# One attention stage, three orders: the rotation ahead of the next root, the second projection behind the first scores, the mask first into its bank

## The chip, the cores and the metric

The kernel runs on one core of a Trainium2 chip. The metric is the device time of one execution in microseconds (us), the median of several runs. A core has five engines that run their own instruction streams and meet at semaphores: TensorE (PE, with its weight loads shown apart as PEld), VectorE (DVE), ScalarE (ACT), GpSimd (POOL) and SyncE (SP), which issues the transfers. TensorE runs at 1.2 or 2.4 GHz; a profile shows which one was granted.

## The reference

The program is a chain of four layers on a sequence of 2048 tokens of width 256: latent attention with 16 heads, a mixture of experts, a gated linear recurrence and a quantized feed-forward layer. The change lies in the attention alone:

```
x_n = layernorm(x)
cq  = rms_norm(x_n @ w_qa.T);  q = cq @ w_qb.T          # 16 heads of 128 + 64
ckv = x_n @ w_kva.T;  k_pe = rope(ckv[..., 64:]);  c = rms_norm(ckv[..., :64])
k_nope, v = split(c @ w_kvb.T)
scores = (q_full @ k_full.T) * scale;  scores[causal] = -inf
y = softmax(scores) @ v @ w_o.T
```

Both norms divide by a root of a mean square, and `rope` rotates pairs of columns by tabled sines and cosines.

## The kernel before

The tokens are 16 tiles of 128. The first stage (lines 160 to 540) makes, for eight pairs of tiles, the normalized latents in transposed form, split into a high and a low part, and beside that the products of weights that later stages use. The second stage is attention itself. Both stages write their order down as a list called `plan`. Every engine walks the same list and does its own share of each entry, in list order, so an entry's place in the list is its place on every engine's queue.

First stage. The list is built in slots s = 0 to 10. For pair n the entries are `xn` (DVE normalizes the inputs, n = s + 1), `x_turn` (PE transposes, ACT copies out, n = s), `latents` (PE multiplies with the latent weights, L483; ACT sums squares, L270 and L272; POOL takes the root in `rms`, L339 and L341; n = s - 1), `latn` (DVE multiplies by the root, L419 and L422; POOL rotates the keys in `rope`, L350 to L357, and splits in `split`, L362 and L364; n = s - 2) and `turned` (PE transposes the latents, L493 to L495; ACT and DVE split them; n = s - 3). `stats` (DVE, L394 and L397) serves four tiles. `unit` entries are twelve weight products: PE multiplies, ACT copies, DVE subtracts (L433, L437, L450, L451); `in_slot` says how many stand in which slot and `bank_of` which PSUM bank each uses. A unit waits until the one before it in its bank has been subtracted. `wqp` in slot 7 is a pair of wide scalings on ACT and a pair of wide subtractions on DVE. On POOL, `split` is followed for pairs 1 and 3 by `fold` (L369), which scales a weight that the units need. PE's `turned` waits for the rotated keys.

Second stage. A group is one query tile with four heads, 64 groups in all; groups of a late and an early tile alternate. `project` (five products L662 into bank pQ, ACT copies out at L760, POOL rotates at L849 to L856) and `turn` (four transposes L669, ACT L764, DVE L879) make a group's queries. `scores` is a chunk of up to 512 keys: three products (L683, L684, L688) into one of four banks, where in a head's last chunk, the diagonal one, a 128-column product of an identity with a mask (L686) adds the causal mask. DVE takes the maximum (L892), ACT the exponential (L772), which frees the bank. `probs` transposes (L701) and `values` multiplies with the values (L743 to L745, 65 columns each). There are 256 diagonal chunks, one for each tile and head; in the four earliest tiles a head has that one chunk only.

Of the kernel before, what the change touches and what calls it, by code (L numbers as in the profile page):

```python
# [25 lines left out]
P = 128  # L26
# [48 lines left out]
def build(nc, x, w_lat, w_qn, w_qpe, w_kn, w_v, w_o, q_ln, kv_ln, cos2, sin2, gw, wg, wu, wd, sel,  # L75
          l_in, l_gate, l_b, l_lam, qg, qu, qd, sg, su, sd, out):
    with ExitStack() as whole:
        sems = {}

        def sem(name):  # L80
            if name not in sems:
                sems[name] = whole.enter_context(nc.semaphore(name))
            return sems[name]
# [9 lines left out]
        def sb(ctx, name, shape, dt=F32, side="left"):  # L93
            return ctx.enter_context(nc.sbuf_tensor(own(name), shape, dt, side=side))

        def sbr(ctx, name, shape, dt=F32):
            return sb(ctx, name, shape, dt, "right")

        def ps(ctx, name, shape, dt=F32):
            return ctx.enter_context(nc.psum_tensor(own(name), shape, dt))  # L100
# [21 lines left out]
        with ExitStack() as first_use:  # L122
            lT_hi = sb(first_use, "lT_hi", [P, 3, T], F32R)
            lT_lo = sb(first_use, "lT_lo", [P, 3, T], F32R)
# [5 lines left out]
        identb = sb(whole, "identb", [P, P], BF16)  # L130
        maskb = sb(whole, "maskb", [P, P], BF16)
# [35 lines left out]
        with ExitStack() as att:  # L167
# [10 lines left out]
            with ExitStack() as pre:  # L178
                NPR = NT // 2
# [12 lines left out]
                latn = sbr(pre, "latn", [P, 3, 2, LAT])  # L192
# [8 lines left out]


                units = [("vo", j) for j in range(H // 2)] + [("wq", 0), ("wq", 1), ("wq", 2), ("wq", 3)]
                in_slot = {5: 1, 6: 1, 7: 1, 8: 2, 9: 3, 10: 4}
                plan = [("stats", 0), ("xn", 0)]
                n_units = 0
                for s in range(NPR + 3):
                    if s % 2 == 0 and s // 2 + 1 < NT // 4:
                        plan.append(("stats", s // 2 + 1))
                    if s + 1 < NPR:  # L210
                        plan.append(("xn", s + 1))
                    if s < NPR:
                        plan.append(("x_turn", s))
                    if 3 <= s:
                        plan.append(("turned", s - 3))
                    if 1 <= s <= NPR:
                        plan.append(("latents", s - 1))
                    if 2 <= s <= NPR + 1:
                        plan.append(("latn", s - 2))
                    if s == 7:  # L220
                        plan.append(("wqp", 0))
                    for _ in range(in_slot.get(s, 0)):
                        plan.append(("unit", n_units))
                        n_units += 1
                assert n_units == len(units)

                bank_of = [0, 0, 0, 0, 1, 2, 3, 0, 1, 2, 3, 0]
                ubank = [pa[:], pt[:], pl[0][:, 0, :], pl[0][:, 1, :]]
                with nc.Block() as block:

# [302 lines left out]
            with ExitStack() as loop:  # L533
# [15 lines left out]
                pS = [ps(loop, f"pS{b}", [P, BT]) for b in range(4)]  # L549
# [9 lines left out]
                tile_at = lambda p: tiles_in_order[groups[p // HG][0]]  # L559

                chunk = [(p, c, min(4, tile_at(p) + 1 - 4 * c)) for p in range(NP) for c in range(tile_at(p) // 4 + 1)]
                first = [next(n for n, k in enumerate(chunk) if k[0] == p) for p in range(NP)] + [len(chunk)]
# [1 line left out]
                LAG = 2  # L564


                plan = [("project", 0), ("turn", 0), ("project", 1)] + [("scores", k) for k in range(first[1])]
                later = []
                sums_due = []

# [34 lines left out]
                for p in range(1, NP):  # L605
                    n = first[p + 1] - first[p]
# [30 lines left out]
                with nc.Block() as block:  # L637

                    @block.tensor
                    def _(pe):  # L640
# [31 lines left out]
                        def scores(at):  # L672
                            p, c, n = chunk[at]
                            i, h = divmod(p, HG)
                            if c == 0:
                                pe.wait_ge(sem("q_hi"), i + 1)
                                pe.wait_ge(sem("q_lo"), i + 1)
                            if at >= 4:
                                pe.wait_ge(sem("exped"), at - 3)
                            w = max(256, n * P)  # L680
                            o, ks = pS[at % 4][:, 0:w], slice(c * BT, c * BT + w)
                            q_hi, q_lo = (q[:, i % 2, h * P:(h + 1) * P] for q in (qT_hi, qT_lo))
                            pe.matmul(o, q_hi, lT_hi[:, 2, ks], start=True, stop=False)  # L683
                            pe.matmul(o, q_hi, lT_lo[:, 2, ks], start=False, stop=False)  # L684
                            if c == tile_at(p) // 4:
                                pe.matmul(pS[at % 4][:, (n - 1) * P:n * P], identb[:], maskb[:], start=False, stop=False,  # L686
                                          skip_group_check=True)
                            pe.matmul(o, q_lo, lT_hi[:, 2, ks], start=False, stop=True).then_inc(sem("scored"), 1)  # L688

                        def bank_t(step):  # L690
                            n = t_index[step]
# [39 lines left out]
                        def values(at):  # L731
# [7 lines left out]
                            for k in range(n):  # L739
# [6 lines left out]
                            m.then_inc(sem("valued"), 1)  # L746

                        steps = {"project": project, "turn": turn, "scores": scores, "probs": probs, "values": values,
                                 "o_turn": o_turn, "sum": sum_, "x_turn": x_turn}
                        for step, at in plan:  # L750
# [398 lines left out]
        c = whole.enter_context(ExitStack())  # L1149
# [20 lines left out]
        with ExitStack() as banks:  # L1170
# [70 lines left out]
            plan = [("up", 0), ("up", 1), ("gate", 0), ("split", 0), ("gate", 1)] + [step for slot in slots for step in slot]  # L1241
# [458 lines left out]
```

## Time and profile before

| | |
|---|---|
| median of 3 runs | 1726.22 us (1725.79 to 1726.46) |
| profiled execution | 1726.31 us, of which the span of the trace is 1724.6 us |
| first stage, until the second one's first product | 99.36 us |
| second stage | 99.36 to about 1240 us |
| TensorE busy in the span | 1571.8 us, 91% |

A time in the profile is in us from the start of the span; a mean duration is in ns where it says so. The start of a row tells when an instruction began; what stands in brackets is the idle time of its engine before it and what ended it. TensorE's rows overlap, since products are pipelined, so the distance from one start to the next tells what a product costs. A row of the timeline merges neighbours of a line, their number stands behind the x.

### The profile page before, as it was taken

What the parts mean: (1) busy time and instruction counts of PE and PEld (TensorE: products, weight loads), DVE (VectorE), ACT (ScalarE), POOL (GpSimd) and SP (SyncE); (2) the same over time, 40 slices, a digit from 0 to 9 for tenths busy, and PEclk for the clock granted to TensorE, in tenths of its full rate; (3) what the DMA queues carried; (4) which work ended last, traced back from release to release, by engine and by line L of the source; (5) the groups of instructions that cost most, each with busy time, mean ns of one, the idle gap of its engine ahead of it and who ended that gap; (6) DMA issues with size and microseconds to landing.
All of it is one profiled execution on the core that took longest, in us unless ns stands there. A gap on an engine that the chain in (4) does not pass through costs nothing. (4 is left out here: it accounts for less than half of the span.)

```text
span 1724.6 us, 38029 instructions
## 1 busy us (share of the span) xinstructions
PE 1571.8 (91%) x14452; PEld 1328.2 (77%) x14452; DVE 1184.3 (69%) x2472; ACT 1021.2 (59%) x2009; POOL 307.3 (18%) x752
## 2 busy tenths in 40 slices
PE   5679999999999899999999999999938999988997
PEld 3458877788888778888888888888826878866886
DVE  3347777777777677788778778778755547476564
ACT  2336665666666566667667667667624455555573
POOL 4411111112111211121211121121010002020231
PEclk8789999999999999999999999999968999999999
DMA  7000000000000000000000000000012100000000
GB/s 217 1 1 2 2 2 1 2 2 1 2 2 2 2 2 2 1 2 2 2 2 2 2 2 2 2 2 2 2 40 73 49 1 1 1 28 13 1 25 25
DMA packets 27524, 22.47 MB, mean 13 GB/s; under 512 B 9660, under 2 KB 25148, under 8 KB 27220
## 3 DMA queue, kind: packets, MB, share of 16 engines
q1 hardware_dynamic: 27348, 20.05, 4.1%
q8 instruction: 120, 1.97, 0.5%
q14 instruction: 56, 0.46, 0.1%
HBM read 17.95 MB, written 2.10 MB: 12 GB/s over the span
## 5 line engine op out<-in xcount | busy, mean ns | idle before, releaser
L783 ACT ACTIVATE pT_hi<-pT 128x512 f16<-128x512 f32 (+3 forms) x640 | 341.5, 534 | 303.6 <-PE pT L701 302.2
L904 DVE TENSOR_TENSOR pT_lo<-pT,pT_hi 128x512 f16<-128x512 f32 (+3 forms) x640 | 387.8, 607 | 148.5 <-ACT pT_hi L783 141.6
L772 ACT ACTIVATE pr<-pS,nmx 128x512 f32<-128x512 f32 (+3 forms) x640 | 401.0, 627 | 25.8 <-DVE nmx L895 24.0
L892 DVE TENSOR_REDUCE cmx<-pS 128x1 f32<-128x512 f32 x576 | 339.2, 617 | 64.0 <-PE pS L688 59.0
L701 PE MATMUL pT<-ident,pr 128*128 128x128 f32 x2176 | 347.3, 276 | 16.4 <-DVE pT_lo L904 15.1
L701 PEld LDWEIGHTS pT<-ident,pr 128*128 128x128 f32 x2176 | 251.9, 140 | 48.7 <-ACT pr L772 24.5
L743 PE MATMUL pO<-c_hi,pT_hi 128*128 128x65 f16 x2176 | 265.6, 194 | 18.5 <-DVE O L922 17.8
L683 PE MATMUL pS<-lT_hi,qT_hi 128*128 128x512 f32 (+2 forms) x640 | 265.5, 415 | 3.1 <-ACT pr L772 3.1
L744 PE MATMUL pO<-c_lo,pT_hi 128*128 128x65 f16 x2176 | 266.4, 193 | 0.0
L745 PE MATMUL pO<-c_hi,pT_lo 128*128 128x65 f16 x2176 | 263.7, 192 | 0.0
L688 PE MATMUL pS<-lT_hi,qT_lo 128*128 128x512 f32 (+2 forms) x640 | 255.8, 400 | 0.0
L1307 PE MATMUL pGU<-lT_hi,W_all 128*128 128x512 f32 (+1 forms) x640 | 220.4, 403 | 16.1 <-ACT sgb L1387 12.1
L684 PE MATMUL pS<-lT_lo,qT_hi 128*128 128x512 f32 (+2 forms) x640 | 234.5, 366 | 0.0
L743 PEld LDWEIGHTS pO<-c_hi,pT_hi 128*128 128x128 f16 x2176 | 205.9, 97 | 28.6 <-ACT pT_hi L783 20.6
L744 PEld LDWEIGHTS pO<-c_lo,pT_hi 128*128 128x128 f16 x2176 | 204.1, 98 | 6.6
L745 PEld LDWEIGHTS pO<-c_hi,pT_lo 128*128 128x128 f16 x2176 | 205.3, 97 | 0.0
L1307 PEld LDWEIGHTS pGU<-lT_hi,W_all 128*128 128x128 f32 (+1 forms) x640 | 121.1, 189 | 47.3 <-ACT sgb L1387 16.3
L849 POOL TENSOR_TENSOR qt<-qs,sn 128x128 f32<-128x128 f32 x64 | 29.2, 457 | 687.5 <-ACT qs L760 687.5
L688 PEld LDWEIGHTS pS<-lT_hi,qT_lo 128*128 128x128 f32 x640 | 123.8, 193 | 16.7
L683 PEld LDWEIGHTS pS<-lT_hi,qT_hi 128*128 128x128 f32 x640 | 120.7, 189 | 16.8 <-ACT pr L772 2.9
L684 PEld LDWEIGHTS pS<-lT_lo,qT_hi 128*128 128x128 f32 x640 | 122.0, 191 | 11.0
L1307 PE MATMUL pGU<-lT_lo,W_all 128*128 128x512 f32 (+1 forms) x320 | 127.3, 398 | 0.0
(268 smaller groups left out, 2484.6 us busy)
## 6 DMA issues: line engine op xcount, KB each, us to landing
X<-in_x SPq DMA_DIRECT2D x4, 512.0 KB, 6.8
wo<-in_w_o SPq DMA_DIRECT2D x1, 2048.0 KB, 10.9
out<-X SPq DMA_DIRECT2D x8, 256.0 KB, 2.0
raw<-in_wd SPq DMA_DIRECT2D x14, 128.0 KB, 2.1
raw<-in_wg SPq DMA_DIRECT2D x13, 128.0 KB, 2.7
raw<-in_wu SPq DMA_DIRECT2D x13, 128.0 KB, 2.7
wqn<-in_w_qn SPq DMA_DIRECT2D x1, 1536.0 KB, 16.1
raw<-in_qg SPq DMA_DIRECT2D x6, 128.0 KB, 2.5
```

The costliest lines, as they stand in the source:

```text
L683: pe.matmul(o, q_hi, lT_hi[:, 2, ks], start=True, stop=False)
L684: pe.matmul(o, q_hi, lT_lo[:, 2, ks], start=False, stop=False)
L688: pe.matmul(o, q_lo, lT_hi[:, 2, ks], start=False, stop=True).then_inc(sem("scored"), 1)
L701: m = pe.transpose(o[:, k * P:(k + 1) * P], pr[:, at % RING, k * P:(k + 1) * P], ident[:])
L743: pe.matmul(o, hi, c_hi[:, j, 0:KVL + 1], start=(j == 0), stop=False)
L744: pe.matmul(o, hi, c_lo[:, j, 0:KVL + 1], start=False, stop=False)
L745: m = pe.matmul(o, lo, c_hi[:, j, 0:KVL + 1], start=False, stop=(j == tile_at(p)))
L772: act.activation(pr[:, at % RING, 0:n * P], pS[at % 4][:, 0:n * P], ACT.Exp, bias=nmx[:, p % 4:p % 4 + 1]).then_inc(sem("exped"), 1)
L783: act.activation(pT_hi[:, a % 4, 0:chunk[a][2] * P], src, ACT.Copy).then_inc(sem("t_hi"), 1)
L892: ch.inc(dve.tensor_reduce(cmx[:, p % 2, c:c + 1], pS[at % 4][:, 0:n * P], AX.X, ALU.max))
L904: dve.tensor_tensor(pT_lo[:, a % 4, 0:w], src, pT_hi[:, a % 4, 0:w], ALU.subtract).then_inc(sem("t_lo"), 1)
L1307: mm = pe.matmul(pGU[bank % 3][0:r, :], W_all[:, m, 2 * g + i, k * P:k * P + r], xT[j][:, k, ts], start=(q == 0), stop=(q == 5))
```

## The change

Three edits. In the first stage the entry `latn` of pair s - 2 moves from behind `latents` to the front of its slot; one unit moves from slot 10 to slot 4, with the banks renumbered. In the second stage `project` of group 1 moves behind the scores of the first head. In a diagonal chunk the mask's product comes first and opens the bank; the three others add to it.

```diff
-                in_slot = {5: 1, 6: 1, 7: 1, 8: 2, 9: 3, 10: 4}
+                in_slot = {4: 1, 5: 1, 6: 1, 7: 1, 8: 2, 9: 3, 10: 3}
                 for s in range(NPR + 3):
+                    if 2 <= s <= NPR + 1:
+                        plan.append(("latn", s - 2))
                     if s % 2 == 0 and s // 2 + 1 < NT // 4:
...
                     if 1 <= s <= NPR:
                         plan.append(("latents", s - 1))
-                    if 2 <= s <= NPR + 1:
-                        plan.append(("latn", s - 2))
...
-                bank_of = [0, 0, 0, 0, 1, 2, 3, 0, 1, 2, 3, 0]
+                bank_of = [0, 0, 0, 0, 0, 1, 2, 3, 0, 1, 2, 3]
...
-                plan = [("project", 0), ("turn", 0), ("project", 1)] + [("scores", k) for k in range(first[1])]
+                plan = [("project", 0), ("turn", 0)] + [("scores", k) for k in range(first[1])] + [("project", 1)]
...
-                            pe.matmul(o, q_hi, lT_hi[:, 2, ks], start=True, stop=False)
-                            pe.matmul(o, q_hi, lT_lo[:, 2, ks], start=False, stop=False)
-                            if c == tile_at(p) // 4:
-                                pe.matmul(pS[at % 4][:, (n - 1) * P:n * P], identb[:], maskb[:], start=False, stop=False,
+                            diagonal = c == tile_at(p) // 4
+                            if diagonal:
+                                pe.matmul(pS[at % 4][:, (n - 1) * P:n * P], identb[:], maskb[:], start=True, stop=False,
                                           skip_group_check=True)
-                            pe.matmul(o, q_lo, lT_hi[:, 2, ks], start=False, stop=True).then_inc(sem("scored"), 1)
+                            pe.matmul(o, q_hi, lT_hi[:, 2, ks], start=not diagonal, stop=False, skip_group_check=diagonal)
+                            pe.matmul(o, q_hi, lT_lo[:, 2, ks], start=False, stop=False, skip_group_check=diagonal)
+                            pe.matmul(o, q_lo, lT_hi[:, 2, ks], start=False, stop=True, skip_group_check=diagonal).then_inc(sem("scored"), 1)
```

On POOL in slot 2 of the first stage, where `ss` to `rr` is a root, `rt` and `latn` the rotation, `c_hi` and `c_lo` the split, and `rs` the deviation of the inputs:

```order
 L339 TENSOR_SCALAR ss<-ss 128x4
 L341 TENSOR_TENSOR rr<-ss,mhalf 128x2x2
+L350 TENSOR_TENSOR rt<-latn,sn 128x2x32
+L351 TENSOR_TENSOR rt<-latn,sn 128x2x32
+L353 TENSOR_TENSOR latn<-latn,cs 128x2x32
+L354 TENSOR_TENSOR latn<-latn,cs 128x2x32
+L356 TENSOR_TENSOR latn<-latn,rt 128x2x32
+L357 TENSOR_TENSOR latn<-latn,rt 128x2x32
+L362 CAST c_hi<-latn 128x2x64
+L364 TENSOR_TENSOR c_lo<-latn,c_hi 128x2x64
 L332 TENSOR_SCALAR rs<-mv 128x4
 L334 TENSOR_TENSOR rs<-rs,mhalf 128x4
```

Pair 0's rotation and split now stand directly behind pair 0's root, where before the root of pair 1 came first; every later pair is moved in the same way.

TensorE where the second stage begins, before, from the transposes of group 0's queries on (the products before them are group 0's projection):

```order
L669 MATMUL pQ<-ident,qs 128x128 x4
L662 MATMUL pQ<-W_hi,lT_hi 128x512
L662 MATMUL pQ<-W_lo,lT_hi 128x512
L662 MATMUL pQ<-W_hi,lT_lo 128x512
L662 MATMUL pQ<-W_1,lT_hi 128x512
L662 MATMUL pQ<-W_1,lT_lo 128x512
L683 MATMUL pS_1<-lT_hi,qT_hi 128x512
```

and in the change, from the first head's diagonal chunk on (three full chunks stand between the transposes and it):

```order
L685 MATMUL pS_1<-maskb,identb 128x128
L687 MATMUL pS_1<-lT_hi,qT_hi 128x512
L688 MATMUL pS_1<-lT_lo,qT_hi 128x512
L689 MATMUL pS_1<-lT_hi,qT_lo 128x512
L662 MATMUL pQ<-W_hi,lT_hi 128x512
L662 MATMUL pQ<-W_lo,lT_hi 128x512
L662 MATMUL pQ<-W_hi,lT_lo 128x512
L662 MATMUL pQ<-W_1,lT_hi 128x512
L662 MATMUL pQ<-W_1,lT_lo 128x512
L687 MATMUL pS_1<-lT_hi,qT_hi 128x512
L688 MATMUL pS_1<-lT_lo,qT_hi 128x512
L689 MATMUL pS_1<-lT_hi,qT_lo 128x512
```

Group 1's projection has changed places with the first head's scores, and stands between the first and the second head.

TensorE at a diagonal chunk of an early tile, behind the products with the values, before:

```order
L745 MATMUL pO<-c_hi,pT_lo 128x65
L683 MATMUL pS_1<-lT_hi,qT_hi 128x256
L684 MATMUL pS_1<-lT_lo,qT_hi 128x256
L686 MATMUL pS_1<-maskb,identb 128x128
L688 MATMUL pS_1<-lT_hi,qT_lo 128x256
L701 MATMUL pT_1<-ident,pr 128x128 x4
```

and in the change:

```order
L746 MATMUL pO<-c_hi,pT_lo 128x65
L685 MATMUL pS_1<-maskb,identb 128x128
L687 MATMUL pS_1<-lT_hi,qT_hi 128x256
L688 MATMUL pS_1<-lT_lo,qT_hi 128x256
L689 MATMUL pS_1<-lT_hi,qT_lo 128x256
L702 MATMUL pT_1<-ident,pr 128x128 x4
```

The mask's product has moved from the third place to the first; from here on every line of the program is one higher.

## Rows read from the trace of the kernel before

**Rows 1.** The page's part on engines: busy us, share of the span, instructions.

```profile
PE 1571.8 (91%) x14452; PEld 1328.2 (77%) x14452; DVE 1184.3 (69%) x2472; ACT 1021.2 (59%) x2009; POOL 307.3 (18%) x752
```

**Rows 2.** Windows: stretch, length, PE, PEld, DVE, ACT, POOL busy, clock, DMA share, GB/s.

```profile
30.00:60.00 30.00, 19.78 (x68) 13.01 (x67) 9.04 (x21) 9.58 (x40) 17.09 (x35) 0.77 0.18 42
130.00:680.00 550.00, 512.10 (x5590) 442.08 (x5587) 406.48 (x809) 352.72 (x697) 90.47 (x216) 1.00 0.01 2
680.00:1240.00 560.00, 550.50 (x6111) 479.94 (x6108) 445.58 (x955) 383.30 (x760) 100.50 (x240) 1.00 0.01 2
```

**Rows 3.** Timeline of slots 5 to 7, first stage: start, duration, instruction.

```profile
46.50 4.87 PE L483 MATMUL pl<-wl,xnT 128*128 128x384 f32 x8
...
51.83 0.20 ACT L272 ACTIVATION_READ_ACCUMULATOR junk<-pl 128x1 f32 x1
...
52.40 1.02 POOL L341 TENSOR_TENSOR rr<-ss,mhalf 128x4 f32<-128x4 f32 x1
...
55.23 0.32 POOL L357 TENSOR_TENSOR latn<-latn,rt 128x64 f32<-128x64 f32 x1
...
55.65 0.30 PE L493 MATMUL pk<-ident,latn 128*128 128x128 f32 x1 [2.98 <-issue]
...
56.33 2.75 PE L483 MATMUL pl<-wl,xnT 128*128 128x384 f32 x8
...
63.82 4.44 PE L483 MATMUL pl<-wl,xnT 128*128 128x384 f32 x8
```

**Rows 4.** Timeline of slots 2 to 8, what starts and bounds them.

```profile
19.68 0.42 DVE L419 TENSOR_TENSOR latn<-pl,rr 128x256 f32<-128x256 f32 x1 [3.48 <-POOL rr L341]
...
26.07 4.85 PE L483 MATMUL pl<-wl,xnT 128*128 128x384 f32 x8
...
35.57 2.35 POOL L369 TENSOR_TENSOR wv<-wv,kln 128x1024 f32<-128x1024 f32 x1
...
75.51 4.03 PE L483 MATMUL pl<-wl,xnT 128*128 128x384 f32 x8
```

**Rows 5.** Timeline from slot 7 to the second stage's first product.

```profile
72.36 1.28 DVE L437 SCALAR_TENSOR_TENSOR W<-wqp,qln,W 64x1024 fp32r<-64x1024 f32 x1
...
88.56 0.27 PE L493 MATMUL pk<-ident,latn 128*128 128x128 f32 x1
...
97.23 0.76 DVE L437 SCALAR_TENSOR_TENSOR W<-pa,qln,W 64x512 fp32r<-64x512 f32 x1 [1.03 <-ACT W L297]
...
99.36 0.77 PE L662 MATMUL pQ<-W_hi,lT_hi 128*128 128x512 f32 x1 [2.89 <-PEq L105]
```

**Rows 6.** Timeline of the second stage's beginning.

```profile
108.03 0.77 PE L662 MATMUL pQ<-W_hi,lT_hi 128*128 128x512 f32 x1 [1.50 <-DVE qT_lo L879]
...
110.54 0.60 ACT L760 ACTIVATE qs<-pQ 128x512 f32<-128x512 f32 x1 [3.38 <-PE pQ L662]
...
113.53 0.46 POOL L856 TENSOR_TENSOR qs<-qs,qt 128x128 f32<-128x128 f32 x1
...
115.22 0.69 ACT L772 ACTIVATE pr<-pS,nmx 128x512 f32<-128x512 f32 x1 [4.09 <-DVE nmx L895]
...
116.82 0.60 PE L669 MATMUL pQ<-ident,qs 128*128 128x128 f32 x4
```

**Rows 7.** Timeline of TensorE at a diagonal chunk; the last such row.

```profile
138.81 0.36 PE L683 MATMUL pS<-lT_hi,qT_hi 128*128 128x256 f32 x1
139.01 0.28 PE L684 MATMUL pS<-lT_lo,qT_hi 128*128 128x256 f32 x1
139.13 0.23 PE L686 MATMUL pS<-maskb,identb 128*128 128x128 bf16 x1
139.17 0.36 PE L688 MATMUL pS<-lT_hi,qT_lo 128*128 128x256 f32 x1
139.37 0.49 PE L701 MATMUL pT<-ident,pr 128*128 128x128 f32 x3
...
1201.10 0.48 PE L683 MATMUL pS<-lT_hi,qT_hi 128*128 128x512 f32 x1
```

## The prediction, made before the changed kernel ran

> **What bounds the kernel now.** I read the page first: TensorE is busy for 91% of the span, the next engine for 69% [rows 1]. That is an average, so the windows come next. In the second stage TensorE is busy 512 of 550 us in its first half and 550.5 of 560 in its second, at a granted clock of 1.00, the 2.4 GHz level [rows 2]. There TensorE is the limit, with some 38 us of idle time in the first half. In the first stage it is not: from 30 to 60 us it is busy 19.8 of 30 us, at a mean clock of 0.77, and no other engine is busier than 17.1 us [rows 2]. Nobody is full, so something there goes round in a ring.
>
> The timeline shows the ring [rows 3]. The reader should follow one slot: the latents start at 46.50 (8 products, 4.87 us); ACT has the squares at 52.03; POOL has the root at 53.42; then the rotation, until 55.55; at 55.65 PE starts the transposes, and at 56.33 the next latents. The rotation is that of the pair before: its own inputs were there a slot earlier, but in POOL's queue it stands behind a root that needs this slot's squares. So one slot costs 5.53 (latents and squares) + 1.39 (root) + 2.13 (rotation) + 0.78 (hand-over and transposes) = 9.83 us, one after the other. The next slot, 56.33 to 63.82, is the same ring with the latents in 2.75 instead of 4.87 us: 7.49 us. From slot 3 (26.07) to slot 8 (75.51 [rows 4]) five slots take 49.4 us.
>
> **The change, part by part.** *Rotation ahead of the next root.* The rotation of pair n now follows its own root and DVE's product with it (0.42 us [rows 4]), and no longer waits for the squares of pair n + 1. The dependences still close, but over two slots: latents and squares 5.53, root 1.39, DVE product 0.42, some 0.5 where that product stands behind a unit's subtractions, rotation 2.13, transposes 0.78: 10.75 us for two slots, 5.4 each. With the short latents, 5.53 becomes 7.49 - 1.39 - 2.13 - 0.78 = 3.19, and the ring 4.2 us a slot.
>
> Then another limit shows. TensorE's work in the window 30 to 60 is 19.8 us for three slots, 6.6 each at clock 0.77 [rows 2], hence 5.1 if all of it ran at the upper level and 10.2 if all at the lower. POOL's 17.1 us hold two folds of 2.35 [rows 4], so some 4.1 us a slot, under TensorE. I take 6.4 us a slot: TensorE almost without gaps, at a mean clock near 0.8, a little above today's, since its gaps of 3 us [rows 3] get shorter.
>
> DVE pays at the front. Its product with the root stands ahead of the statistics and the normalization in its queue. In slot 2 that product starts at 19.68 [rows 4] and both halves end near 20.7; the statistics of four tiles and the normalization of pair 3, done before it until now, follow it: some 2.6 us in all by my estimate, until 23.3. Behind that queue wait PE's transposes of the inputs (0.6), those of pair 0 (1.3) and the latents of slot 3, which I put at 25.2, against 26.07. Slot 7 begins at 25.2 + 4 x 6.4 = 50.8, against 63.82 [rows 3].
>
> Slot 7 holds the wide scalings. Before, DVE ended them at 73.64 [rows 5], 9.8 us after slot 7's latents began. Behind them on DVE now stand a unit's subtractions (0.85) and the product for pair 6; behind that POOL's rotation waits (2.1), and behind that PE's transposes: 50.8 + 9.8 + 0.85 + 0.42 + 2.1 = about 64. The root of pair 7 stands behind that rotation and its split in POOL's queue, so the last transposes come another 0.8 + 1.39 + 0.42 + 2.13 = 4.7 later, at 68.7. What follows took 99.36 - 88.56 = 10.8 us [rows 5] with four weight units; now there are three, and the one taken out, which moved into slot 9's wait, saves at most (97.23 - 88.56)/4 = 2.2; I take 1.9. The second stage then starts at 68.7 + 8.9 = 77.6 instead of 99.36: **22 us**. The moved first unit (slot 4) runs on PE where the 6.4 already counts it; its inputs need the fold, 2.35 us on POOL, now also a slot earlier, which I hold hidden; if that cover is gone, it is 2 us once. Bounds: with 5.1 us a slot the gain is 27 us, with 9 it is 12. No transfer binds: DMA is at 0.18 in the window 30 to 60 [rows 2], after which it carries nothing here.
>
> *Projection behind the scores.* Before, group 1's projection starts at 108.03, ACT copies it at 110.54, POOL has rotated it at 113.99, and PE transposes at 116.82; the first exponential starts at 115.22 [rows 6]. Now the four chunks of scores start at 108.03. They took from 110.30 to 114.1; with the low clock over more of them they end near 113.0. The projection follows, until about 114.2, and its copy ends near 114.9. ACT's queue has that copy ahead of the first exponential, which therefore begins at 114.95 instead of 115.22: nearly nothing won. The rotation takes 113.99 - 111.14 = 2.85 us after the copy and now ends at 117.75, so PE's transposes slip from 116.82 to 117.8. Behind them on PE and ACT wait the first transposes of probabilities and all further exponentials. That is a **loss of 1.0 us**; it lies between -0.3 (only the exponential counts) and +1.4.
>
> *Mask first.* The starts [rows 7] tell what a product costs. The first product behind a 65-column one takes 0.20 us to the next start, the second 0.12, the mask 0.04, the third, behind the mask, again 0.20. So a float32 weight load lies open for 0.08 us when the product ahead is short, and it is hidden behind a long one. Before, an early tile's diagonal chunk pays twice: behind the values and behind the mask. Now the mask's load, half as long, meets the short product, and one open load remains, behind the mask. Where a long product is ahead (the chunk before in the same head) the sum stays the same: one open load in either order. I count 76 of the 256 diagonal chunks behind short products in the trace, the first at 138.81, the last at 1201.10 [rows 7]. 76 x 0.08 = 6.1 us is the upper bound; below it is 0, should the mask's own load lie open instead, and less than 0 only for the rival below. Three quarters of these chunks lie in the first half, where TensorE idles 38 us of 550 and a faster PE partly just waits longer. I take half, **3 us**.
>
> One rule of the Trainium skill would make it nothing: the page "TensorE: Matmul & The Clock Gate", section "The mechanism" of its part on packing small matmuls, lists that a weight load overlaps products in flight only when the row group differs. All products here use all rows, so no load would hide and no place would be better: 3 us less gain, 1705. The distances of 0.12 against 0.20 us speak against it.
>
> Sum, against the profiled execution: 1726.31 - 22 + 1 - 3 = 1702.3. That execution lies 0.1 us from the median 1726.22, so the forecast is **1702 us**.
>
> **The rivals.** (a) The denser work does not lift TensorE's clock, or it falls for longer in the waits around the wide scalings. At 9 us a slot the first stage gains 12 us: 1726.3 - 12 + 1 - 3 = 1712, and up to 1716 without the mask's share. For it speaks that the clock was 0.77 with TensorE busy for two thirds. (b) The clock goes the other way, all slots at 5.1 us: 27 us, and the whole mask share of 6: 1694. The skill's page named above says in its table on why this matters for kernels that idle gaps between bursts of products lower the clock; shorter gaps would then mean more time at 2.4 GHz. (c) The mask brings nothing: 1705. It lies within my range. (d) The stage's gain is hidden or replaced: DVE's queue, where the product with the root now stands ahead of the normalization, feeds a new ring of one slot (root, product, normalization, transposes, latents). Worked out, that path needs 1.39 + 0.42 + 0.68 + 1.8 + 0.7 + 0.6 us behind the squares in the slots with statistics and has a whole slot for it, so I give it little: about 1726. (e) Slower: opening the bank with a 128-column product makes the wide product that adds onto it dearer. Above (22 - 1)/256 = 0.08 us for each of 256 chunks, the same size as the open load, it eats the gain. The second and third product add onto a bank already and take 0.12 us for 256 columns [rows 7], which speaks against it.
>
> **How the numbers follow.** A measurement of this kernel can tell about 0.2%, 3.5 us. The main case, with its mask share anywhere from 0 to 6, gets 0.74 and runs from 1695 to 1709; (a) 0.12, (b) 0.08, (d) 0.03, (e) 0.03. The range 1691 to 1713 takes in (b) and most of (a). Faster by over 0.2%: 0.95; within 0.2%: 0.03; slower: 0.02.
>
> **What would show it.** The second stage's first product near 77 us; starts of L483 six to seven us apart in slots 3 to 7; POOL's rotation directly behind DVE's product; near the beginning of the second stage the transposes L669 of group 1 about 9.8 us after the projection or scores begin; at early tiles the distances 0.04, 0.20, 0.12, 0.12. The prediction is wrong if the slots keep 9 us or more, if the exponentials do not slip with the transposes, or if the wide scalings of slot 7 move the end by more than 3 us against the 64 worked out.

## The result, and the profile after

The changed kernel takes 1701.31 us in the median of 4 runs (1700.4 to 1701.61), the one before 1726.01 in the runs beside it. The ratio is 0.9864, its 95% interval 0.9852 to 0.9877: 24.7 us less, where 24 were forecast. The profiled execution of the changed kernel took 1701.13 us with a span of 1699.4, against 1724.6.

The page of the changed kernel, the part on engines:

```profile
PE 1560.8 (92%) x14452; PEld 1309.5 (77%) x14452; DVE 1182.0 (70%) x2472; ACT 1020.6 (60%) x2009; POOL 306.5 (18%) x752
```

TensorE is 11 us less busy, though it does the same 14452 products. The mean granted clock of the whole execution rose from 0.972 to 0.977, so more of the products run at the upper level; how much of the 11 us that explains was not taken apart. Windows of the changed kernel (stretch, length, busy us of PE, PEld, DVE, ACT and POOL, granted clock, DMA share, GB/s):

```profile
30.00:60.00 30.00, 24.04 (x98) 15.89 (x97) 19.74 (x46) 17.54 (x65) 22.18 (x53) 0.94 0.17 40
88.00:94.00 6.00, 2.93 (x16) 1.75 (x14) 1.52 (x4) 1.98 (x4) 2.59 (x6) 1.00 0.00 0
95.00:101.00 6.00, 6.00 (x21) 4.64 (x22) 2.46 (x6) 1.76 (x4) 0.00 (x0) 0.50 0.00 0
```

Against [rows 2], all engines do more in the same 30 us of the first stage, and TensorE's clock there is 0.94 instead of 0.77. The third line is a surprise: in the second stage, after a stretch at full clock, TensorE fell once more to 0.50.

The first stage's timeline in the changed kernel, which answers to [rows 3 to 5]:

```profile
24.64 3.43 PE L483 MATMUL pl<-wl,xnT 128*128 128x384 f32 x8
...
28.30 2.36 POOL L369 TENSOR_TENSOR wv<-wv,kln 128x1024 f32<-128x1024 f32 x1
...
29.00 2.75 PE L483 MATMUL pl<-wl,xnT 128*128 128x384 f32 x8
...
31.02 1.02 POOL L341 TENSOR_TENSOR rr<-ss,mhalf 128x4 f32<-128x4 f32 x1
...
32.07 0.42 DVE L419 TENSOR_TENSOR latn<-pl,rr 128x256 f32<-128x256 f32 x1 [4.38 <-POOL rr L341]
...
33.01 1.39 DVE L394 BATCH_NORM_STATS2 stats<-X 128x6 f32<-128x256 f32 x4
...
34.74 0.81 DVE L407 TENSOR_SCALAR xn<-X,mv,rs 128x256 f32<-128x256 f32 x2
...
35.60 0.66 PE L472 MATMUL pt<-ident,xn 128*128 128x128 f32 x4 [3.00 <-DVE xn L407]
...
37.39 3.88 PE L483 MATMUL pl<-wl,xnT 128*128 128x384 f32 x8
...
43.06 2.75 PE L483 MATMUL pl<-wl,xnT 128*128 128x384 f32 x8
...
44.12 1.02 POOL L341 TENSOR_TENSOR rr<-ss,mhalf 128x4 f32<-128x4 f32 x1
...
45.17 0.42 DVE L419 TENSOR_TENSOR latn<-pl,rr 128x256 f32<-128x256 f32 x1 [1.34 <-POOL rr L341]
...
45.68 0.32 POOL L350 TENSOR_TENSOR rt<-latn,sn 128x64 f32<-128x64 f32 x1 [0.54 <-DVE latn L419]
...
47.38 0.32 POOL L357 TENSOR_TENSOR latn<-latn,rt 128x64 f32<-128x64 f32 x1
...
48.48 2.75 PE L483 MATMUL pl<-wl,xnT 128*128 128x384 f32 x8
...
53.09 2.75 PE L483 MATMUL pl<-wl,xnT 128*128 128x384 f32 x8
...
60.03 0.30 PE L493 MATMUL pk<-ident,latn 128*128 128x128 f32 x1 [0.53 <-issue]
...
64.64 0.30 PE L493 MATMUL pk<-ident,latn 128*128 128x128 f32 x1 [0.30 <-issue]
...
73.68 0.66 PE L662 MATMUL pQ<-W_hi,lT_hi 128*128 128x512 f32 x1 [2.89 <-PEq L105]
```

Read the starts of L483. Slot 3 begins at 24.64, slot 4 at 29.00, slot 5 at 37.39, slot 6 at 43.06, and slots 7 and 8 follow at 48.48 and 53.09. So slots 5, 6 and 7 take 5.7, 5.4 and 4.6 us, where five slots before took 9.9 us each in the mean. At 44.12 POOL takes a root; half a microsecond after its end DVE has multiplied, and POOL goes straight on to rotate. The one long slot is the fourth, 8.4 us: POOL's fold at 28.30 stands ahead of the root of 31.02, DVE's product waits for that root, and behind the product wait the statistics and the normalization, for which PE waits 3.00 us at 35.60. The second stage starts at 73.68 instead of 99.36: 25.7 us earlier.

The beginning of the second stage, which answers to [rows 6], and a diagonal chunk of an early tile behind a short product, which answers to [rows 7]:

```profile
90.28 0.47 PE L687 MATMUL pS<-lT_hi,qT_hi 128*128 128x512 f32 x1 [1.36 <-ACT pr L773]
...
92.53 0.63 PE L669 MATMUL pQ<-ident,qs 128*128 128x128 f32 x4 [1.31 <-POOL qs L857]
...
94.91 0.80 PE L687 MATMUL pS<-lT_hi,qT_hi 128*128 128x512 f32 x1 [1.32 <-ACT pr L773]
...
114.05 0.48 PE L662 MATMUL pQ<-W_hi,lT_hi 128*128 128x512 f32 x1
...
151.64 0.22 PE L685 MATMUL pS<-maskb,identb 128*128 128x128 bf16 x1
151.67 0.36 PE L687 MATMUL pS<-lT_hi,qT_hi 128*128 128x256 f32 x1
151.87 0.28 PE L688 MATMUL pS<-lT_lo,qT_hi 128*128 128x256 f32 x1
151.99 0.28 PE L689 MATMUL pS<-lT_hi,qT_lo 128*128 128x256 f32 x1
...
1229.29 0.28 PE L728 MATMUL pQ<-Wvo_hi,OT_lo 128*128 128x256 f32 x1
```

Group 1's transposes start 92.53 - 73.68 = 18.9 us after the stage's first product, before 116.82 - 99.36 = 17.5: PE waits 1.31 us for POOL's rotation. At the early tile the four products now stand 0.03, 0.20, 0.12 apart: one open weight load where there were two, since the mask's product now follows the short product after 0.03.

Three places divide the change: the stage's first product, the projection of group 2 (in the kernel before at 135.92) and the last product of the last sum of heads (before at 1255.02). The second and the third of these rows of the kernel before are

```profile
135.92 0.48 PE L662 MATMUL pQ<-W_hi,lT_hi 128*128 128x512 f32 x1
...
1255.02 0.28 PE L727 MATMUL pQ<-Wvo_hi,OT_lo 128*128 128x256 f32 x1
```

From start to group 2 the kernel before takes 36.6 us and the changed one 114.05 - 73.68 = 40.4, so the head of the stage is 3.8 us longer. From there to the last sum it is 1119.1 against 1229.29 - 114.05 = 1115.2: 3.9 us shorter. The rest of the program takes 469.56 and 470.11 us. Sum, with two decimals: -25.68 + 3.82 - 3.87 + 0.55 = -25.2 us, the difference of the spans.

### The profile page after: what moved, and what is told of

Its sections match the earlier page's. It is cut to its first block and busy times, and to the rows that moved or that the text cites. A ratio compares the mean times of both kernels' runs of the same rounds, so it can differ in the third digit from the quotient of the medians.

```text
span 1699.4 us, 38029 instructions
## 1 busy us (share of the span) xinstructions
PE 1560.8 (92%) x14452; PEld 1309.5 (77%) x14452; DVE 1182.0 (70%) x2472; ACT 1020.6 (60%) x2009; POOL 306.5 (18%) x752
## 5 line engine op out<-in xcount | busy, mean ns | idle before, releaser
L687 PE MATMUL pS<-lT_hi,qT_hi 128*128 128x512 f32 (+2 forms) x640 | 281.5, 440 | 4.2 <-ACT pr L773 2.7
L689 PE MATMUL pS<-lT_hi,qT_lo 128*128 128x512 f32 (+2 forms) x640 | 235.8, 368 | 0.0
## 6 DMA issues: line engine op xcount, KB each, us to landing
wqn<-in_w_qn SPq DMA_DIRECT2D x1, 1536.0 KB, 16.3
```

Of the source, the lines that this page charges most:

```text
L687: pe.matmul(o, q_hi, lT_hi[:, 2, ks], start=not diagonal, stop=False, skip_group_check=diagonal)
L689: pe.matmul(o, q_lo, lT_hi[:, 2, ks], start=False, stop=True, skip_group_check=diagonal).then_inc(sem("scored"), 1)
```

## The experiments

Single executions of the kernel before lay between 1721.07 and 1731.01 us in these comparisons, so differences of a few us are read in the traces, at the three places above. Each kernel has one trace, and a trace, too, is one execution. Three figures tell how far traces of the same code lie apart. Seven kernels below and above have the changed kernel's whole first stage, and their second stage starts between 73.33 and 75.48 us. From group 2 to the last sum the traces with the mask third take 1118.8 to 1119.1 us and those with it first 1115.0 to 1115.4. The rest of the program, the same code in all, takes 469.1 to 472.1. So the middle part tells a few tenths of a us, and the start of the second stage only some 2 us.

**1. The three edits apart.** The first kernel has the first stage's edit alone; against the changed kernel, projection and mask are put back:

```diff
-plan = [("project", 0), ("turn", 0)] + [("scores", k) for k in range(first[1])] + [("project", 1)]
+plan = [("project", 0), ("turn", 0), ("project", 1)] + [("scores", k) for k in range(first[1])]
...
-                            pe.matmul(o, q_hi, lT_hi[:, 2, ks], start=not diagonal, stop=False, skip_group_check=diagonal)
+                            pe.matmul(o, q_hi, lT_hi[:, 2, ks], start=True, stop=False)
```

> The first stage's edit alone (with the moved unit), projection and mask as before. Theory: the first stage gives all of the gain, its second stage starts 25.7 us earlier (73.7 instead of 99.4) and nothing else moves: about 1700.3 us. Rival: the parts depend on one another, since the earlier start shifts where TensorE's clock rises at the head of the second stage; then the second stage itself would be 2 to 4 us longer than before, as in the changed kernel, and the time near 1703.

Measured: 1703.6 us (1700.46 to 1708.04), ratio 0.9867 (0.983 to 0.9903). The second stage starts at 74.06. But its head is 39.4 us long, though projection and mask are as before. The window shows why:

```profile
92.00:98.00 6.00, 4.74 (x16) 3.66 (x15) 2.77 (x4) 2.93 (x5) 0.00 (x0) 0.50 0.00 0
```

The clock fell again, as in the changed kernel, and without the projection's move. The rival was right on this point. From group 2 to the last sum it takes 1119.0 us, as before. The execution shown is one of the two long ones: four executions of this kernel took 1700.46, 1700.89, 1706.31 (this one) and 1708.04 us, the first two at a mean clock of 0.980 and 0.981, the others at 0.975. Some of its 5.8 us above the fastest lie behind the last sum, where this trace takes 472.1 us and most others 469 to 470.

The second kernel is the changed one with only the projection back:

```diff
-plan = [("project", 0), ("turn", 0)] + [("scores", k) for k in range(first[1])] + [("project", 1)]
+plan = [("project", 0), ("turn", 0), ("project", 1)] + [("scores", k) for k in range(first[1])]
```

> The changed kernel with group 1's projection back at its old place. Theory: in the changed kernel the projection's move costs 3.8 us by group 2, of which 1.4 us is the wait for its rotation and 2.4 us the clock, which fell to 1.2 GHz again behind that wait; both go, and the time is about 1697.5 us. Rival 1: the clock falls there whatever the projection does, since the stage begins at another moment: 1699.9. Rival 2: the 3.8 us belong to the mask's place: 1701.3 as it is.

Measured: 1696.79 us (1696.64 to 1699.98), ratio 0.9834 (0.981 to 0.9859). The stage's head takes 35.3 us, group 1's transposes start 16.3 us into it, and the clock does not fall a second time. From group 2 to the last sum it takes 1115.3 us. This kernel is 4.5 us faster than the changed one in the medians: the second of the three edits was a loss. The head is shorter than the 36.6 us before although its order is the same. In this execution the clock was still at the upper level when the stage began; in other kernels with this order and the mask first that began it at the lower level it takes up to 36.8.

The third kernel is the changed one with the mask back in third place:

```diff
-                            if diagonal:
-                                pe.matmul(pS[at % 4][:, (n - 1) * P:n * P], identb[:], maskb[:], start=True, stop=False,
-                                          skip_group_check=True)
...
+                            if c == tile_at(p) // 4:
+                                pe.matmul(pS[at % 4][:, (n - 1) * P:n * P], identb[:], maskb[:], start=False, stop=False,
+                                          skip_group_check=True)
```

> The changed kernel with the mask's product at its old place, third. Theory: the mask's place gives 3.9 us spread over the diagonal chunks behind short products, so the time is about 1705.2 us, and the second stage's lag of 3.8 us at group 2 stays to its end. Rival: the lag is made up by idle time that the pipeline has anyway, the mask's place gives nothing: 1701.3 us.

Measured: 1704.92 us (1702.03 to 1705.77), ratio 0.9874 (0.9846 to 0.9902). From group 2 on it takes 1118.9 us, so the mask's place is what gives the 3.7 us there. Its head, with the projection moved, shows the projection's own price, since here the clock stayed up (the profiled execution is the fastest of four, the others took 2.5 to 3.7 us more):

```profile
92.00:98.00 6.00, 4.23 (x26) 3.42 (x27) 3.32 (x5) 3.03 (x6) 0.31 (x1) 1.00 0.00 0
...
92.45 0.63 PE L669 MATMUL pQ<-ident,qs 128*128 128x128 f32 x4 [1.31 <-POOL qs L856]
...
94.84 0.50 PE L683 MATMUL pS<-lT_hi,qT_hi 128*128 128x512 f32 x1 [1.31 <-ACT pr L772]
```

The same wait of 1.31 us stands there, and group 2 begins 37.9 us into the stage, 1.3 more than before.

The fourth kernel is the one before with the projection's move alone, the line of the second kernel the other way round.

> The kernel before with the projection's move alone. Theory: slower by the wait of 1.4 us and, if the clock falls again behind it as in the changed kernel, by 2.4 us more: 1727.4 to 1729.8 us. Rival, the forecast's own sizing: 1.0 us, 1727.0. Rival 2: the pipeline makes it up, 1726.0.

Measured: 1727.42 us against 1727.75, ratio 1.0004 (0.9986 to 1.0022): too small for the runs. In the trace the head takes 39.4 us, 2.9 more than before, with one more stretch at the lower clock. So the projection's price is 1.3 us where the clock holds, and more where it falls. The clock's second fall is not its effect alone: one trace without the move shows it, one with the move does not.

**2. Whose queue it was.** In the fifth kernel only POOL's order changes; DVE multiplies at the slot's end as before:

```diff
                     if 2 <= s <= NPR + 1:
-                        plan.append(("latn", s - 2))
+                        plan.append(("rotate", s - 2))
...
                         plan.append(("latents", s - 1))
+                    if 2 <= s <= NPR + 1:
+                        plan.append(("latn", s - 2))
...
-                            elif what == "latn":
+                            elif what == "rotate":
                                 rope(n)
```

> The changed kernel (projection at its old place) with the edit on POOL alone: POOL rotates pair s - 2 at the head of slot s, DVE's product with the root stays at the slot's end. Theory: the gain of the first stage comes from POOL's queue, where the rotation no longer stands behind the next root; DVE's place is free. What closes is rotation, transposes, copy and low part, product, rotation, about 5 us a slot: the second stage starts at 73 to 76 us. Rival: DVE's place is half of it, since its product then stands behind the low part of the pair before; 7 us a slot, start near 83.

In the sixth kernel only DVE's order changes: `latn` stands at the head of the slot and `rotate` behind `latents`.

> The counterpart: DVE's product at the head of the slot, POOL's rotation at its old place behind the next root. Theory: the ring of one slot stands, 10.2 us a slot at 1.2 GHz and 7.5 at 2.4; the second stage starts at 96 to 99 us, where the 2 us are the moved unit's. Rival: the queue of DVE was the cause, start near 74.

Measured: 1700.39 us (1699.46 to 1701.33) with POOL's order and 1719.93 us (1718.91 to 1722.15) with DVE's; ratios 0.9856 (0.9833 to 0.9878) and 0.9976 (0.9961 to 0.9991). These two have the mask first and the projection at its old place. The latents of slots 2 and 3 and the first product of the second stage with POOL's order, then that product with DVE's:

```profile
17.94 2.75 PE L485 MATMUL pl<-wl,xnT 128*128 128x384 f32 x8
23.08 2.75 PE L485 MATMUL pl<-wl,xnT 128*128 128x384 f32 x8
...
77.54 0.77 PE L664 MATMUL pQ<-W_hi,lT_hi 128*128 128x512 f32 x1 [2.89 <-PEq L105]
```

```profile
95.19 0.76 PE L664 MATMUL pQ<-W_hi,lT_hi 128*128 128x512 f32 x1 [2.89 <-PEq L105]
```

With POOL's order the stage ends 21.8 us sooner than before, with DVE's 4.2. Both kernels have the moved unit, whose 1.8 us (below) are in each of these numbers. So POOL's order alone brings 20.0 of the 25.7 us and DVE's alone 2.4; what the two bring only together, 25.7 - 20.0 - 2.4 - 1.8 = 1.5 us, is within what traces of the same code differ by. So the ring was closed in POOL's queue, as read. Neither expectation was met quite: the start of the fifth kernel lies 1.5 us behind its range, since DVE's product there stands behind the low part of the pair before and slots 3 to 6 take 6.2 to 7.1 us; the start of the sixth lies 0.8 us ahead of its range, its clock from 30 to 60 being 0.89.

**3. The clock's share.** The seventh kernel is the one before, with the transposes of the inputs of pairs 3 to 7 issued five times over:

```diff
-                            for q in range(2):
-                                for k in range(KD):
-                                    m = pe.transpose(pt[:, (2 * q + k) * P:(2 * q + k + 1) * P], xn[:, n % 2, q, k * P:(k + 1) * P], ident[:])
+                            for again in range(1 if n < 3 else 5):
+                                for q in range(2):
+                                    for k in range(KD):
+                                        m = pe.transpose(pt[:, (2 * q + k) * P:(2 * q + k + 1) * P], xn[:, n % 2, q, k * P:(k + 1) * P], ident[:])
```

> The kernel before, with the transposes of the inputs of pairs 3 to 7 issued five times over (the same results written again), so that TensorE is busy in most of the 3 us in which it waits for the rotation. Theory: a part of the first stage's gain of 25.7 us is the clock; with it at 2.4 GHz a slot takes 7.5 us instead of 9.8 to 10.2, for about three slots: second stage starts at 91 to 93 us instead of 99.4. Rival: the clock is not what stretches those slots, or filler delays the ring itself: 99 us or later.

Measured: 1719.02 us (1718.93 to 1719.33), ratio 0.9964 (0.9951 to 0.9977). Its window and the start of its second stage:

```profile
30.00:60.00 30.00, 24.11 (x127) 18.36 (x128) 11.06 (x24) 11.97 (x47) 18.85 (x41) 0.94 0.18 41
...
90.59 0.77 PE L663 MATMUL pQ<-W_hi,lT_hi 128*128 128x512 f32 x1 [2.89 <-PEq L105]
```

Useless work makes the kernel faster. The clock is 0.94 as in the changed kernel, the ring of one slot stands (starts at 24.71, 32.20, 40.53, 49.32, 56.80, so 7.5 to 8.8 us a slot), and the stage ends 8.8 us sooner, 0.4 us ahead of the range expected. Of the 8.8 us, 0.7 lie ahead of the first repeated transposes (slot 2's latents start at 17.15 instead of 17.88) and are not theirs. About 8 of the first stage's 25.7 us can thus be had from the clock alone; some 16 need the order, and 1.8 are the moved unit's.

**4. The head of the second stage.** The eighth kernel is the second one with 22 transposes of the identity, into a bank that nobody reads yet, where TensorE waits:

```diff
                             m.then_inc(sem("projected"), 1)
+                            if i == 0:
+                                for again in range(16):
+                                    pe.transpose(pT[1][:, 0:P], ident[:], ident[:])
...
                             m.then_inc(sem("q_turned"), 1)
+                            if i == 0:
+                                for again in range(6):
+                                    pe.transpose(pT[1][:, 0:P], ident[:], ident[:])
```

> The changed kernel with the projection at its old place and 22 transposes of the identity into a bank that nobody reads, 16 behind the first projection and 6 behind the first group's transposes, where TensorE waits for the rotation and for the split of the queries. Theory: the clock's fall at the head of the second stage (10 to 20 us at 1.2 GHz) costs 2 to 4 us; with TensorE busy it rises near the fifth us of the stage: group 2's projection at 32 to 33 us after the stage's start instead of 35.3, and 1694 us. Rival: the filler makes the group's own work wait or the clock does not rise sooner: 1696.8 or more.

Measured: 1696.04 us (1694.47 to 1698.25), ratio 0.9832 (0.9816 to 0.9849). Windows of the changed kernel and of the second one, which both lack these transposes:

```profile
74.00:87.00 13.00, 7.89 (x21) 5.26 (x21) 2.62 (x4) 1.20 (x2) 2.58 (x6) 0.50 0.00 0
```

```profile
77.00:85.00 8.00, 3.10 (x9) 2.38 (x10) 0.69 (x1) 1.02 (x2) 2.59 (x6) 0.50 0.00 0
```

and of this one:

```profile
74.00:77.00 3.00, 2.97 (x9) 2.43 (x10) 0.00 (x0) 0.58 (x1) 0.00 (x0) 0.53 0.00 0
78.00:84.00 6.00, 3.94 (x26) 3.20 (x24) 0.69 (x1) 1.04 (x2) 1.73 (x4) 1.00 0.00 0
```

The clock is up from 78 us on, where in the second kernel it is still low at 85, and the head takes 34.1 us. That is 1.2 us less than the second kernel's 35.3, not the 2 to 3 expected. But the two did not begin alike: the second kernel's first products ran at the upper level and this one's at the lower (0.53 from 74 to 77). The kernel of part 5 with early tiles alone has the same order, also began at the lower level, and its head takes 36.7 us. So the filler is worth 1.2 to 2.6 us, and these traces do not tell it closer. In the medians the 0.8 us between the two are within the spread. These two and the kernel with early tiles alone (1696.48) are the fastest of all, 5 us under the changed kernel.

**5. Where the mask's gain lies.** Two kernels on the basis of the second one have the mask first only in some tiles. The line that differs between them is

```diff
+                            early = tile_at(p) < 4
+                            if diagonal and not early:
...
```

in the one, and `early = tile_at(p) >= 4` in the other; where `early` is false the mask stands third.

> The changed kernel with the projection at its old place, and the mask first only in the four earliest tiles, where a head has one chunk: 64 diagonal chunks, 61 of them behind a short product. From group 2's projection to the last sum of heads the kernels with the mask third take 1118.75 to 1119.11 us, those with it first 1115.03 to 1115.37. Theory, the open weight load behind a short product: most of the 3.7 us remain, since these hold 61 of the 76 such chunks: 1115.8 us (the lag shrank by 3.1 us in the groups with them). Rival, that the first product adds onto the mask's bank and the third is free of it in every diagonal chunk alike: a quarter of the gain, 1118.

> The counterpart: mask first in the twelve late tiles only, 192 diagonal chunks, 15 of them behind short transposes, the others behind a long product. Theory: 0.7 us of the 3.7, so 1118.3 us from group 2's projection to the last sum. Rival, alike in every chunk: three quarters of the gain, 1116.2.

Measured between group 2's projection and the last sum, first the early tiles:

```profile
110.05 0.48 PE L662 MATMUL pQ<-W_hi,lT_hi 128*128 128x512 f32 x1
...
1226.08 0.28 PE L736 MATMUL pQ<-Wvo_hi,OT_lo 128*128 128x256 f32 x1
```

then the late ones:

```profile
110.86 0.48 PE L662 MATMUL pQ<-W_hi,lT_hi 128*128 128x512 f32 x1
...
1229.36 0.28 PE L736 MATMUL pQ<-Wvo_hi,OT_lo 128*128 128x256 f32 x1
```

That is 1116.0 and 1118.5 us. Against the 1118.9 us that kernels with the mask third take in the mean, the 64 chunks of early tiles hold 2.9 of the 3.7 us and the 192 others 0.4. The whole times are 1696.48 and 1701.47 us. The gain does not go by the number of diagonal chunks. It does not go by the 76 short products either, once they are taken apart: 58 of them are products with the values, all in early tiles, and 18 are transposes. Behind transposes the mask's own load lies open. The rows show it, the kernel before first, then the changed one:

```profile
723.92 0.62 PE L669 MATMUL pQ<-ident,qs 128*128 128x128 f32 x4
724.29 0.36 PE L683 MATMUL pS<-lT_hi,qT_hi 128*128 128x256 f32 x1
```

```profile
698.62 0.60 PE L669 MATMUL pQ<-ident,qs 128*128 128x128 f32 x4
699.06 0.22 PE L685 MATMUL pS<-maskb,identb 128*128 128x128 bf16 x1
```

In the kernel before, the chunk's first product starts 0.37 us after the start of the four transposes, in the changed one 0.44. From the start of the product ahead to the start of the one behind, a chunk behind the values takes 0.594 us before and 0.497 after (256 columns), one behind transposes 0.596 and 0.576. Early tile and product with the values ahead go together here, so the two kernels alone do not part them; the rows do.

**6. The moved unit.** The last kernel has the units in their old slots and banks:

```diff
-                in_slot = {4: 1, 5: 1, 6: 1, 7: 1, 8: 2, 9: 3, 10: 3}
+                in_slot = {5: 1, 6: 1, 7: 1, 8: 2, 9: 3, 10: 4}
```

> The changed kernel with the projection at its old place and the twelve weight units in their old slots and banks (none in slot 4, four in slot 10). Theory: the moved unit saves the step of one unit in the tail, 1.8 us: the second stage starts at 75.5 to 76.8 us instead of 73.7 to 75.0. Rival: the slot the unit fills was free only because another stands still there, and the start is the same.

Measured: 1698.58 us (1697.66 to 1699.49). Its last transposes and the second stage's start:

```profile
64.64 0.30 PE L493 MATMUL pk<-ident,latn 128*128 128x128 f32 x1 [1.16 <-POOL latn L357]
...
75.47 0.77 PE L662 MATMUL pQ<-W_hi,lT_hi 128*128 128x512 f32 x1 [2.89 <-PEq L105]
```

The last transposes start at 64.64 as in the changed kernel, and the stage behind them at 75.47 instead of 73.68: the unit's step is 1.8 us in the tail, as 1.9 was forecast. All traces bear this out: from the start of the last transpose (L495) to the second stage it is 8.47 us in the nine with the moved unit and 10.25 or 10.26 in the four without. That the unit costs nothing in slot 4 is less sure, since the last transposes of kernels with the same first stage start up to 2.1 us apart.

## Why the prediction was right, point by point

**The ring.** Right. The rotation stood behind a root that it did not need, and taking it out of that place on POOL alone brought 20.0 us, the moved unit's 1.8 aside. The forecast put slots 3 to 7 at 6.4 us; they took (48.48 - 24.64)/4 = 6.0, and behind the fourth slot 5.7, 5.4 and 4.6. So the term "6.4 us a slot, TensorE almost without gaps at a clock near 0.8" was too dear: the clock was 0.94, of which the seventh kernel shows the worth. Rival (b), the clock goes up with the denser work, was half true. In the last of these slots POOL was the limit: its roots at 48.80 and 53.41 stand 4.6 us apart, the 4.1 that the forecast gave POOL's own work and 0.54 in which it waits for DVE's product.

**DVE's front.** Slot 3 began at 24.64, forecast 25.2; traces of the same first stage have it between 24.3 and 25.7. That the front costs something is shown by the kernel with POOL's order alone: its slot 2 took 23.08 - 17.94 = 5.1 us, against 24.64 - 17.18 = 7.5 here, so 2.3 us for the 2.6 estimated. Some 0.6 of the 2.3 are the clock: pair 0's six transposes at the slot's end stand 0.21 us apart here and 0.11 there. The forecast said of the fold "which I hold hidden; if that cover is gone, it is 2 us once". The cover was gone: POOL's 2.36 us lay ahead of a root, DVE's product waited for it, the statistics and the normalization behind it kept PE for 3.00 us, and slot 4 took 8.4 us instead of about 6. A second fold, at 41.40, delayed a root too and cost PE next to nothing. That is the path of rival (d), in one slot only.

**The wide scalings.** Forecast 13.2 us from slot 7's latents to the transposes of pair 6, measured 60.03 - 48.48 = 11.6. The 9.8 us taken from the kernel before held a stretch at the lower clock. The next two terms were right: 4.7 us to the last transposes, measured 4.6, and 8.9 us from there to the second stage, measured 9.0. Altogether 25.7 us gained where 22 were forecast; by the other traces with this first stage, 23.9 to 26.0.

**The projection.** The mechanism was right and its size nearly: 1.0 us forecast, 1.3 measured in the stage's head where the clock held. Group 1's transposes started 92.53 - 82.23 = 10.3 us after the scores began instead of 9.8, since the low clock lay over nearly all of the scores. The head of the stage was 3.8 us longer in the profile, and the 2.5 us beyond are a stretch at 0.50 that the forecast did not have.

**The mask.** 3 us forecast, 3.7 to 3.9 measured, at the places forecast. The forecast priced all 76 chunks behind short products at 0.08 us. The 58 behind products with the values save 0.096 each: one load less lies open, and the step between the mask's product and its neighbour is 0.03 us where it was 0.04. The 18 behind transposes save 0.02, since there the mask's own load lies open, the case that the forecast named as its lower bound. Together they could give 5.9 us, not 6.1, and 3.7 arrive. So the bound was right by two errors that cancel. The Trainium skill's rule of the page "TensorE: Matmul & The Clock Gate", section "The mechanism", that a weight load overlaps products in flight only when the row group differs, would have left nothing to gain. With that rule the trace disagrees: starts are 0.12 us apart behind a long enough product and 0.20 behind a short one, all on 128 rows.

That the sum came within 1 us is partly luck, because errors cancelled: the forecast had 3.7 us too little gain in the first stage and 2.8 us too little cost at the second one's head. It also took 3.5 us for what a measurement can tell, while executions of the kernel before later lay 10 us apart.

## What to carry to other kernels

Where no engine is full and the slots are long, follow one item through every queue and look for the entry that waits in a queue behind something it does not need; one such place here held 20 us. A wait costs twice when it lets TensorE's clock fall, so a reordering may return more than its ring says, and the slots of a kernel should be priced at both clock levels. Undo the parts of a change one by one: here one of three edits was a loss that the sum of the others hid. Work moved behind other work is paid at its last consumer: the projection gave the scores a head start of which nothing was left, since the rotation and the transposes came later.

## What was not expected of the hardware

TensorE's clock fell a second time in the head of the second stage in the changed kernel (0.50 from 95 to 101 us), in the first-stage kernel (0.50 from 92 to 98), and shortly in the projection's kernel, but in none of the other traces. The waits ahead of it are nearly the same with it and without: 1.36, 1.31 and 1.32 us in the changed kernel, 1.36, 1.31 and 1.31 in the third kernel of part 1, whose clock stayed up. It cost 2.5 to 2.8 us, in the projection's kernel 1.6. What decides it is open. The first-stage kernel took 1700.5 us in one execution and 1708.0 in another, so it may well be a matter of the execution and not of the kernel; each kernel has one trace, and none varied the moment alone at which the stage begins. The same may be behind the spread of 10 us among executions of one kernel; no trace shows it. And in a kernel bound by a ring, 80 useless transposes made it 6.5 us faster.
